# A two-layer graph network on one core: loops over 521 supertiles instead of 522, and a single last sum in layer 0

## What is computed

```python
h = relu(layernorm(x))
x = x + segment_sum(h[src] * edge_weight[:, None], dst)       # layer 0
h = relu(layernorm(x)); s, v = h[:, :8], h[:, 8:].reshape(n, 8, 3)
w = (relu(edge_attr_32 @ W1 + b1) @ W2 + b2).reshape(e, 4, 8, 8)
# layer 1: messages m0 (8) and m1 (8 x 3) per edge from s[src], v[src],
# edge_attr_4 and w; summed over dst, plus a product of s and v with si_w0, si_w1
x = x + layer1(h, src, dst, edge_attr_4, edge_attr_32)
```

## Time and profile before

| | |
|---|---|
| median of 3 runs | 6243.72 us (6241.42 to 6246.52) |
| the profiled execution | 6246.71 us |
| its span, first to last instruction | 6244.9 us |
| busy: PE, DVE, POOL, ACT | 97%, 89%, 75%, 58% |
| granted TensorE clock, mean | 0.991 of full |

### The profile page before, as it was taken

The page is one execution under the profiler, slowest core; times in us unless marked ns, Lnnn a source line. Parts: engine busy times, 40 slices in busy tenths (PEclk is TensorE's granted clock), DMA queues, the critical chain, the costliest instruction groups (busy, mean ns, idle before and its releaser), DMA issues.

```text
span 6244.9 us, 161388 instructions
## 1 busy us (share of the span) xinstructions
PE 6088.4 (97%) x44043; PEld 4996.6 (80%) x44043; DVE 5563.4 (89%) x13227; ACT 3634.2 (58%) x14178; POOL 4668.2 (75%) x4915
## 2 busy tenths in 40 slices
PE   6999999999999999996999999999999999999998
PEld 5888888888888888885777777777777777777776
DVE  7888888778777787775999999999999999999999
ACT  3222222222222222224888888888888888888886
POOL 6777777777777777776777777777777777777776
PEclk9999999999999999997999999999999999999998
DMA  4111111111111111112111111112121111111121
GB/s 113 34 32 34 34 33 33 34 34 32 34 32 34 34 32 34 34 33 42 41 40 42 41 40 40 41 42 42 40 43 40 41 42 42 40 43 40 40 43 37
DMA packets 290300, 247.19 MB, mean 40 GB/s; under 512 B 105284, under 2 KB 286740, under 8 KB 289800
## 3 DMA queue, kind: packets, MB, share of 16 engines
q0 software_dynamic: 156256, 80.32, 9.4%
q1 hardware_dynamic: 133212, 163.33, 9.3%
q10 hardware_dynamic: 802, 3.22, 0.2%
HBM read 241.24 MB, written 5.25 MB: 39 GB/s over the span
## 4 chain that ended last, share of the span: by engine, by line
POOL 28%; PE 15%; issue 10%; POOLq 0%; DVE 0%; ACT 0%; DMA 0%; DVEq 0%; ACTq 0%
POOL z L486 28%; PE hp_ps L924 7%; PE w_ps L853 3%; PE sc_ps L877 1%; PE w_ps L842 1%; PE w_ps L850 1%; PE sc_ps L880 1%; PE sc_ps L885 0%; PE w_ps L815 0%; POOLq L483 0%; DMA z<-h_table,idx 0%; POOLq L287 0%; POOLq L484 0%; POOLq L482 0%; DVE x_sb L1187 0%
## 5 line engine op out<-in xcount | busy, mean ns | idle before, releaser
L486 POOL DMA_INDIRECT z<-h_table,idx x4883 | 4635.9, 949 | 1498.2 <-issue 1471.6
L770 PE MATMUL w_ps<-parts,pick 128*128 128x448 f32 x12110 | 2551.4, 369 | 69.3 <-DVE pick L1078 56.7
L770 PEld LDWEIGHTS w_ps<-parts,pick 128*128 128x128 f32 x12110 | 2257.5, 188 | 279.6 <-issue 70.3
L613 ACT ACTIVATE z<-z,squares 128x32 f32<-128x32 f32 x3132 | 726.8, 309 | 2045.0 <-DMA z<-h_table,idx 1933.5
L924 PE MATMUL hp_ps<-parts,pick 128*128 128x448 f32 x7224 | 1601.4, 372 | 0.0
L924 PEld LDWEIGHTS hp_ps<-parts,pick 128*128 128x128 f32 x7224 | 1316.1, 188 | 262.4 <-issue 163.0
L1078 DVE TENSOR_TENSOR pick<-sc_ps,feat 128x896 fp32r<-128x896 f32 x865 | 906.1, 1080 | 4.3 <-DMA feat<-key_table 4.1
L853 PE MATMUL w_ps<-w_sb,squares 64*128 64x256 f32 x6264 | 842.9, 378 | 0.0
L853 PEld LDWEIGHTS w_ps<-w_sb,squares 64*128 64x128 f32 x6264 | 722.8, 187 | 73.0 <-issue 0.3
L1244 DVE TENSOR_TENSOR prod<-w_ps,squares 128x384 f32<-128x384 f32 (+1 forms) x1044 | 778.8, 746 | 0.9 <-ACT squares L674 0.9
L711 ACT ACTIVATE squares<-iota_sb,rel_sb 128x32 f32<-128x32 f32 x3132 | 713.7, 307 | 0.0
(11 more groups left out here) (95 smaller groups left out, 5328.1 us busy)
## 6 DMA issues: line engine op xcount, KB each, us to landing
z<-h_table,idx POOLq DMA_INDIRECT x4883, 2.4
feat<-key_table SPq DMA_DIRECT2D x345, 192.0 KB
squares<-in_ft_sh SPq DMA_DIRECT2D x261, 216.0 KB
feat<-key_table SPq DMA_DIRECT2D x173, 128.0 KB
h_table<-big SPq DMA_DIRECT2D x10, 280.0 KB
rel_sb<-in_dst_t SPq DMA_DIRECT2D x1, 1566.0 KB, 8.6
idx_all<-in_src_t SPq DMA_DIRECT2D x1, 1530.0 KB, 10.1
squares<-in_ew_t SPq DMA_DIRECT2D x1, 1530.0 KB, 14.1
```

The source lines that it names most:

```text
L486: pool.indirect_dma_start(z[:, r, u, :], None, rows, bass.IndirectOffsetOnAxis(ap=idx[:, r, u:u + 1], axis=0)).then_inc(z_in[r], 16)
L613: last = nc.scalar.activation(z[:, r, u, :], z[:, r, u, :], ACT.Copy, scale=ew_all[:, bass.ds(n * G + u, 1)])
L770: mm = pe.matmul(fold_ps[:, pick_banks[k], 0:NC * D], pick[:, k, blk, :], parts[:, t, :, blk, :], start=(blk == 0 and t == 0), stop=(blk = ...
```

## The change

`S`, over which the loops and semaphore counts run, becomes the number of supertiles that hold edges, 521. `ST` keeps 522 for the tables, the keys and the set-up. As 521 is odd, PE's pairs in layer 0 end with a half: the lag becomes 5, and the sum of a supertile that does not exist is skipped. 521 // 6 = 86, so every loop has one turn fewer and five supertiles more are written out behind it.

```diff
-def gnn_two_layers(nc, x, src_t, ...
+def gnn_two_layers(nc, edges, x, src_t, ...
     T = src_t.shape[1]
-    S = T // G
+    ST = T // G
+    S = -(-edges // SUP)
...
-    SPP = largest_divisor(S, 125)
-    SK = S // SPP
+    SPP = largest_divisor(ST, 125)
+    SK = ST // SPP
...
-        base_dram = nc.dram_tensor("base_table", [S], I32).ap()
+        base_dram = nc.dram_tensor("base_table", [ST], I32).ap()
...
-                n, count = b * R0 + r, BATCH if s is None else min(BATCH, S - s)
+                n, count = b * R0 + r, BATCH if s is None else min(BATCH, ST - s)
...
                     for late in (5, 4):
+                        if s is not None and s - late >= S:
+                            continue
                         v = (r - late) % R0
                         pe.wait_ge(msg0_ready, n - late + 1)
                         for u in range(G):
                             mm = pe.matmul(total0_ps[v % 2], z[:, v, u, :], onehot[:, v, u, :],
                                            start=(u == 0), stop=(u == G - 1))
                         mm.then_inc(sum0_ready, 1)
-            supertiles(pe, R0, sum0, lag=4)
+            supertiles(pe, R0, sum0, lag=4 + S % 2)
...
-                whole = s is None or s - r % BATCH + BATCH <= S
+                whole = s is None or s - r % BATCH + BATCH <= ST
...
-                of = extra_row(b, r) + S if e else b * R0 + r
+                of = extra_row(b, r) + ST if e else b * R0 + r
...
-                                        base_bc[:].unsqueeze(2).to_broadcast([P, S, G]),
+                                        base_bc[:].unsqueeze(2).to_broadcast([P, ST, G]),
...
-    gnn_two_layers(nc, *args)
+    gnn_two_layers(nc, E, *args)
```

More of the change, by code:

```diff
@@ L44, in largest_divisor, with gnn_two_layers @@
     return max(k for k in range(1, most + 1) if n % k == 0)
-def gnn_two_layers(nc, x, src_t, src_pe, src_last, dst_flat, dst_t, ew_t, ft_sh, sh_one, w1_2, b1_2, w2_2, si_mat, iota,
+def gnn_two_layers(nc, edges, x, src_t, src_pe, src_last, dst_flat, dst_t, ew_t, ft_sh, sh_one, w1_2, b1_2, w2_2, si_mat, iota,
                    rows, ident, stacked, b2_2, marks, out):
@@ L69, in gnn_two_layers @@
     assert TILE + WIN + GB <= 384 and J % JG == 0 and S // R0 >= 2 and GU >= 2 and J * D - NC * D >= R1 // 2 * (HALF + 2 * G * 4) + 2 * HALF + 2 * G * MUL * 5 + G * WIN
-    assert AW % 2 == 0 and R0 % PERIOD == 0 and NPE == S + EXTRA * (S // PERIOD) and S % R0 == 0 and S % R1 == 0
+    assert AW % 2 == 0 and R0 % PERIOD == 0 and NPE == ST + EXTRA * (ST // PERIOD) and ST % R0 == 0 and ST % R1 == 0
     def gathered_by_pool(r):
@@ L135, in gnn_two_layers @@
         h1_dram = nc.dram_tensor("h1_table", [N, D], F32).ap()
-        base_dram = nc.dram_tensor("base_table", [S], I32).ap()
+        base_dram = nc.dram_tensor("base_table", [ST], I32).ap()
         key_dram = nc.dram_tensor("key_table", [NPE, 1, P], F32).ap()
-        span_dram = nc.dram_tensor("span_table", [S], I32).ap()
+        span_dram = nc.dram_tensor("span_table", [ST], I32).ap()
         w_ps = psum("w_ps", [P, 2, 3, 512])
@@ L175, in gnn_two_layers @@
         rel_sb = sb("rel_sb", [P, T])
-        base_row, span_row = sb("base_row", [1, S], I32), prod_flat[0:1, 8 * WN:8 * WN + S].bitcast(I32)
+        base_row, span_row = sb("base_row", [1, ST], I32), prod_flat[0:1, 8 * WN:8 * WN + ST].bitcast(I32)
         span_max = sb("span_max", [1, 1], I32)
-        base_bc = sb("base_bc", [P, S], I32)
+        base_bc = sb("base_bc", [P, ST], I32)
         least, most = sb("least", [SPP, SK]), sb("most", [SPP, SK])
@@ L400, in load_keys @@
                     sp.dma_start(key[:, extra:extra + EXTRA, :],
-                                 key_dram[bass.ds(extra_row(b, r) + S, EXTRA)].rearrange("s a e -> a s e")
+                                 key_dram[bass.ds(extra_row(b, r) + ST, EXTRA)].rearrange("s a e -> a s e")
                                  .to_broadcast([P, EXTRA, P])).then_inc(keys_in[r // BATCH], 16)
@@ L593, in _ @@
             act.wait_ge(tab_out, 32)
-            nc.scalar.dma_start(base_bc[:], base_dram.rearrange("(a s) -> a s", a=1).to_broadcast([P, S])).then_inc(tab_in, 16)
+            nc.scalar.dma_start(base_bc[:], base_dram.rearrange("(a s) -> a s", a=1).to_broadcast([P, ST])).then_inc(tab_in, 16)
             nc.scalar.dma_start(base_row[:], base_dram.rearrange("(a s) -> a s", a=1)).then_inc(tab_in, 16)
```

## The result

The kernel after took 6211.43 us (median of 12 executions, 6210.42 to 6260.25), the kernel before 6242.57 us (median of 12, 6227.89 to 6278.6; three of the 12 are those of the prediction, the nine new ones alone have a median of 6234.51). The ratio is 0.995, with a 95% interval of 0.9931 to 0.9969. The time is that of the rival "slow stretch gone", 6211.9; "shorter or gone" had 10% together.

The account below looks back on a forecast made before the run. POOL's gather issue was taken to bound both layers, with PE and DVE nearly full in layer 1. Layer drains of 8.44 + 8.9 = 17.3 us, with code at 0, took the median from 6243.7 to 6226.4 us; range 6217 to 6240.

Parts of the forecast that it names:

- slow stretch gone: Rival: layer 1's early stretch at 1.27 us a gather vanishes, a further 14.5 us, giving 6211.9.
- shorter or gone: Rival case: layer 1's slow stretch gets shorter or vanishes; 10%, 6211.9 us if it vanishes.
- The gathers: POOL, both layers: supertile 521's five gathers each go, 6.24 and 6.25 us, 12.5 together.
- Layer 0's drain: End of layer 0: it ends at DVE's addition of supertile 520, not 521; 8.44 us, issue and slow one-row landing included.
- Layer 1's drain: End of layer 1: DVE's last product comes 8.9 us earlier, 520 taking 521's place and 521's DVE work gone.
- my bounds: Layer 1's end: 7.4 us if DVE gained nothing from the missing work, 9.0 if it started with ACT.
- Written-out code: Both layers: five supertiles written out behind loops one turn shorter, taken to cost 0 us.
- The bound of 3 us: Written-out code's upper cost: one POOL wait of 1.6 us for each layer, 3 us.
- the rival with 10: Written-out code stalls POOL or moves a loop: 3 us, 6229.4, up to 10 us if it recurs; 7%.
- Only the issue time counts: Rival: the long landing belongs to any stream's last gather, so 520 inherits it; gain 12.5 us, 6231.2; 10%.
- Layer 1's pace: Rival: layer 1's slow stretch may change: gone 6211.9 us, held throughout 6264; shorter or gone 10%, longer 10%.
- The held gather: Layer 1's slow stretch: one gather in ten, starting 0.05 us after a DVE product, takes 1.28 us, not 0.94.

Follow-up runs that it names:

- e13: Kernel before with layer 0 over 516 supertiles, layer 1 still 522; lowest 6193.95 us, 34.6 under before's lowest.
- e1: Kernel before with the change in layer 0 alone (521, layer 1 at 522); five runs 6234.9 to 6237.49 us, profiled one 6218.61.
- e16: Same kernel as e1, run again on another chip; lowest 6219.15 us, 9.4 under before's lowest, profiled run 6266.26.
- e3: Kernel before, 522 supertiles, padded src indices naming different rows instead of one; lowest 6239.98 us, 3.2 under before's lowest.
- e2: Kernel before with the change in layer 1 alone (521, layer 0 at 522); lowest 6233.47 us, 9.7 under before's lowest.
- e4: Kernel before, all loops in both layers one turn shorter, six more supertiles written out; lowest 6243.31 us, 0.2 above before's lowest.
- e15: Kernel before, only layer 0's loops one turn shorter, six more supertiles written out; lowest 6228.07 us, 0.4 under before's lowest.
- e11: Kernel after, unchanged, on another chip; median 6222.54 us against before's 6239.74, ratio 0.9971.
- e10: Kernel before with two layer 1 DVE products reading one tensor instead of two (output wrong); lowest 6235.97 us, 1.2 under before's lowest.
- e6: Kernel after with six chained memsets on POOL in supertile 5 of layer 1; lowest 6214.15 us, 14.8 under before's lowest.
- e7: Kernel after with twelve chained copies on DVE in supertile 5 of layer 1; lowest 6212.84 us, 16.1 under before's lowest.
- e5: Kernel before with twelve chained copies on DVE in supertile 5 of layer 1; lowest 6229.45 us, 0.5 above before's lowest.
- e12: Kernel before with three chained memsets on POOL in supertile 5 of layer 1; lowest 6240.11 us, 3.0 above before's lowest.
- e14: Kernel before with layer 0 over 520 supertiles, layer 1 still 522; lowest 6213.93 us, 14.6 under before's lowest.

## Why the prediction was right in its sum and wrong in its time

**The gathers: right.** 4873 of them, and 12.5 us of issue; e13's 26 gathers and one padded landing gave 34.6 us, as worked out.

**Layer 0's drain: right.** 8.44 forecast; five gathers of 1.248 and a tail of 5.03 instead of 7.34 us make 8.55, and e1 (its five runs) and e16 gave 8.2 and 9.4 us under before's lowest. There is one addition where there were two, and the single sum waits for nothing new. The reason, indices that name one row, was tested by e3 alone and stands: in its profile the tail is 4.88 us in layer 0 and 13.42 in layer 1 (before: 7.34 and 17.13).

**Layer 1's drain: right in total, its inner step not borne out.** 8.9 forecast, 9.7 lowest to lowest in e2. I had DVE gain 1.6 us of missing work and start 0.7 us behind ACT (6201.1 against 6200.44). In after's profile it starts 1.72 us behind, since in that execution DVE's first products stand 11.1 us behind the gathers of their supertile, where before's, past its slow stretch, stand at 10.5: DVE's own work counts there, and ACT's early scalars bring nothing. In e2's profile it is 0.82 us. From the start of the last gather to the end of the last addition it is 15.32 us against 17.13, in e2's profile 14.41. So of the tail 1.8 or 2.7 us went, with 6.25 of gathers 8.1 or 9.0: both ends of my bounds (7.4 to 9.0) are about what the two ways of running give.

**Written-out code: right.** 0 us taken; e4 +0.2, e15 -0.4 us. The bound of 3 us and the rival with 10 were too cautious. The Trainium skill ("Runtime: NRT & Kernel Launch", section "Instruction fetch mechanics") has straight code prefetched and its crossings mostly hidden, and here the runs agree; its stall for a loop that lies badly was not seen: apart from the place of the added memsets, no idle time ahead of a gather of layer 1 exceeds 0.33 us in any profile.

**"Only the issue time counts": fallen.** It wanted 12.5 us; e11 has 17.2 between the medians, and e3 shows the long landing leave with the indices.

**Layer 1's pace: this step failed.** The prediction said "four executions of the kernel before lie within 5.3 us, so the stretch ends each time within some 50 supertiles of the same place, and layer 1 begins after the change with the same instructions." Nine further executions of the same kernel lie between 6227.89 and 6278.6 us. 50.7 us between them is a stretch that lasts the whole layer (510 supertiles at 0.10 us are 51) against none at all, and e16 shows the two cases in profiles. The first four had met by chance. Nor does a stretch end or begin at a fixed place: in the profiles it ends at supertile 24, 75, 150 or not at all, and in e3 it begins at 493. I read a small spread of few runs as a property of the program, though I had written beside it that a tenth of a us decides. So I weighed two chances of 10% against what should have been near even, and kept 6243.7 as the base with 14.5 us of slow stretch in it, while in after that stretch is mostly missing: 17.3 + 14.5 = 31.8, and 31.1 came. That these two agree so well is partly luck: the median of before falls anywhere in a spread of 50 us, and with its nine new runs alone the difference is 23.1. Firm are the level, for 6227.9 less 17.3 is 6210.6 and ten of the 12 runs of after lie between 6210.42 and 6213.35, and the 17 us of the sum. The mechanism and its price (0.10 us a supertile) were right, the chance was not. The other half, that "the same instructions" begin layer 1, is true and says nothing, for the same program starts either way.

**The held gather: right, and now measured.** The prediction had it decided by a tenth of a us, from two gathers; the table under e10 shows the whole curve, from 0 to 0.41 us. Its "one gather in ten takes 1.28 us" was too round: of 700 gathers in before's slow stretch 55 take over 1.05 us, 1.21 in the mean. The Trainium skill ("GPSIMD Engine Reference", section "Specifications") has GpSimd contend with DVE instructions that have two SBUF inputs. By that half of the rule e10 should hold no gather; it leaves 0.03 to 0.07 us and one gather of 1.18 us, so the runs agree but for this rest. The same row names DVE instructions in a two-port mode as well; no run here shows whether e10's one-input operations are such.

Some signs came otherwise. The place of the change from 1.27 to 1.25 us was to stay near 3870; it is gone. The queue's share was to fall to near 9% and ACT's last idle to about 2 us; they fell to 2.0 and 5.7% and to 1.30 us. The last product of DVE was to come 17.3 us earlier; it comes 19.9 earlier, as the whole execution is shorter. POOL's 0.30 us was to be unbroken, and it is, in the 75 waits that the profile puts to DVE too.

No kernel here was reliably faster than the kernel after; e6 and e7, with a delay added, stand 14.8 and 16.1 us under the lowest of before, where it stands at 17.5 and 16.0.

## What to carry to other kernels

Where two engines run at nearly one pace, as POOL and DVE do here, the kernel may have more than one steady way of running, and the same program may take either: ask for the spread of many runs before you price an edit, and compare the lowest runs as well as the medians. A base time with such a stretch in it is not a base; price the edit against the run without it, and give the stretch its own term with its own chance. Padding indices that all name one row made the gathers slower that read them; spread them, or do not read them. And read how long a wait is before you name its cause: 75 waits for DVE cost no more here than the idle time that stands ahead of every gather.

## What the runs showed of the hardware

- An indirect gather of 128 rows costs POOL 0.944 us and 0.30 us between two, 1.249 us together; but one whole execution can stand at 1.2485 and another of the same kind at 1.2510, with the gather's own time at 0.944 or 0.946 us. Over 2262 gathers that is 5.7 us (e1 and e2, layer 0).
- Five gathers whose 128 indices name one row land 1.45 to 1.72 us apart at the end of layer 0 in before, though they are issued every 1.25, and ACT starts 2.3 us later behind the last of them; the queue's share is 22.0 and 33.8% instead of 2.0 and 5.7%.
- A gather that begins while two adjoining DVE products with two SBUF inputs run is held until some 0.1 us before they end: up to 0.41 us (1.352 instead of 0.944, means of e5's bins). If they begin over about 0.06 us behind the gather's start, it is not held at all. With one input 0.03 to 0.07 us are left.
- Layer 1 runs at three spacings of gathers on this program: 1.27, 1.253 and 1.249 to 1.250 us. The idle time between two is 0.305 us in all three; the gather's own mean length differs (0.963 to 0.965, 0.948 to 0.949, 0.944 to 0.946). All six profiles whose DVE settles 11.1 us behind the gathers (after, e6, e7, e11, e12 and most of e14) have 1.253, those at about 10.4 to 10.6 the one or the other of the lower two.
- How often runs stand out differs between the chips for one and the same kernel: 23 of 29 and 21 of 28 runs over 8 us above the lowest on two of them, 4 of 29 on another.
